# Attention-value matmuls issued between the two score matmuls of each exponential tile

## The reference, cut to what matters

```python
x = x + L0(x)        # a linear layer chosen by item
x = x + L1(x)        # a Laplacian in both directions and a reaction term
# L2, per item and head: 256 queries from the side input, 256 keys from x and one own key
score   = concat([q @ k_prev.T * SCALE (masked), (q * k_self).sum(-1) * SCALE])
weights = softmax(score)
attn    = weights[..., :-1] @ v_prev + weights[..., -1:] * v_self
x = x + attn @ Wo + bo
x = x + L3(x)        # three networks relu(x @ wi) @ wo, mixed by a softmax gate
```

## Time and profile before

| what | us |
|---|---|
| median of 3 runs | 1064.06 |
| lowest and highest run | 1061.18, 1064.1 |
| the profiled execution, its own time | 1063.02 |
| its span, first to last instruction | 1061.2 |

### The profile page before, as it was taken

One profiled execution on the slowest core, in us unless ns is written; L12 is line 12 of the kernel. 1 busy time (PEld: TensorE's weight loads), 2 busy tenths in 40 slices (PEclk: granted clock), 3 DMA queues, 4 the chain that ended last, 5 costly groups with the idle time before them and its releaser, 6 DMA issues.

```text
span 1061.2 us, 27596 instructions
## 1 busy us (share of the span) xinstructions
PE 990.0 (93%) x9488; PEld 931.2 (88%) x9488; DVE 795.0 (75%) x1552; ACT 682.1 (64%) x1435; POOL 616.8 (58%) x548
## 2 busy tenths in 40 slices
PE   5669999999999999999999999999999999999896
PEld 5359999898999989899998989999898999989896
DVE  6576787778878777887877788787778878778633
ACT  5564866667586666748666674866667486666641
POOL 5683747476474747647464664747566474755440
PEclk8669999999999999999999999999999999999988
DMA  6626142522514252251425225142522514251110
GB/s 161 166 83 109 51 70 76 94 80 60 109 50 67 76 96 80 60 109 50 66 77 96 80 59 107 53 64 77 98 80 59 109 51 62 78 98 52 42 50 11
DMA packets 91387, 82.68 MB, mean 78 GB/s; under 512 B 11972, under 2 KB 90852, under 8 KB 91364
## 3 DMA queue, kind: packets, MB, share of 16 engines
q1 hardware_dynamic: 91364, 82.38, 36.1%
HBM read 52.59 MB, written 4.20 MB: 54 GB/s over the span
## 4 chain that ended last, share of the span: by engine, by line
PE 65%; DVE 16%; issue 8%; ACT 7%; POOL 2%; DMA 1%; SPq 1%; DVEq 0%; ACTq 0%
PE hid L550 7%; PE hid L551 6%; PE hid L552 6%; PE out L550 6%; PE out L552 5%; PE out L551 5%; PE front L550 5%; PE front L552 4%; PE front L551 4%; PE front L652 4%; PE front L665 4%; DVE s_max L1034 3%; DVE hid_lo L1118 2%; DVE gate_terms L1133 2%; ACT prob L869 2%
## 5 line engine op out<-in xcount | busy, mean ns | idle before, releaser
L1269 POOL TENSOR_TENSOR prob_lo<-prob,prob_hi 128x512 f16<-128x512 f32 x144 | 175.1, 1216 | 102.9 <-ACT prob_hi L873 102.8
L550 PE MATMUL out<-hid_hi,exp_hi 128*128 128x256 f32 x768 | 228.5, 297 | 4.2 <-DVE hid_lo L1118 4.1
L550 PE MATMUL hid<-x_hi,exp_hi 128*128 128x256 f32 x768 | 230.3, 300 | 1.5 <-DVE x_lo L1114 1.5
L551 PE MATMUL hid<-x_lo,exp_hi 128*128 128x256 f32 x768 | 217.4, 283 | 0.0
L552 PE MATMUL hid<-x_hi,exp_lo 128*128 128x256 f32 x768 | 216.8, 282 | 0.0
L551 PE MATMUL out<-hid_lo,exp_hi 128*128 128x256 f32 x768 | 214.7, 280 | 0.0
L552 PE MATMUL out<-hid_hi,exp_lo 128*128 128x256 f32 x768 | 214.7, 280 | 0.0
L1212 POOL TENSOR_TENSOR exp_lo<-raw,exp_hi 128x512 fp32r<-128x512 f32 x128 | 169.1, 1336 | 70.6 <-ACT exp_hi L890 70.5
L1034 DVE TENSOR_REDUCE s_max<-front 128x2 f32<-128x512 f32 x256 | 167.9, 687 | 42.2 <-PE front L652 40.4
L869 ACT ACTIVATE prob<-front 128x512 f32<-128x512 f32 x256 | 154.2, 603 | 41.0 <-PE front L665 38.1
L1118 DVE SCALAR_TENSOR_TENSOR hid_lo<-hid,hid_hi 128x512 fp32r<-128x512 f32 x192 | 130.8, 681 | 62.8 <-ACT hid_hi L912 61.6
(11 more groups left out here) (166 smaller groups left out, 2266.5 us busy)
## 6 DMA issues: line engine op xcount, KB each, us to landing
raw<-in_wi SPq DMA_DIRECT2D x64, 256.0 KB, 3.8
raw<-in_wo SPq DMA_DIRECT2D x64, 256.0 KB, 2.8
q_rows<-w_raw SPq DMA_DIRECT2D x80, 128.0 KB, 4.0
k_rows<-x1T SPq DMA_DIRECT2D x48, 128.0 KB, 5.0
k_rows<-x_raw SPq DMA_DIRECT2D x48, 128.0 KB, 6.1
x_raw<-in_x SPq DMA_DIRECT2D x16, 256.0 KB, 2.9
w_raw<-in_w SPq DMA_DIRECT2D x16, 256.0 KB, 2.8
s_raw<-in_side SPq DMA_DIRECT2D x16, 256.0 KB, 3.7
```

What stands on the lines that cost most here:

```text
L550: nc.tensor.matmul(acc, w_hi, a_hi, start=first, stop=False)
L551: nc.tensor.matmul(acc, w_hi, a_lo, start=False, stop=False)
L1269: nc.gpsimd.tensor_tensor(prob_lo[:, h % NPROB, :], prob[:, h % NPROB, :], prob_hi[:, h % NPROB, :], ALU.subtract).then_inc(prob_split_poo ...
```

## The change

`attend` is called inside the loop over k, after the first of the two matmuls, and no longer after both. The increment that tells ACT that the head's scores are ready stays on the second matmul, which now comes after the eight matmuls of `attend` and after the waits at its head. The same instructions are issued, and the orders of ACT, DVE, POOL and SP are as before.

```diff
                     for k in range(C):
                         last = nc.tensor.matmul(psum[:, k * S:(k + 1) * S], k_rows[0:ROWS_EXP, h, k * P:(k + 1) * P],
                                                 q_rows[0:ROWS_EXP, h, :], start=True, stop=True)
+                        if k == 0 and h >= BEHIND:
+                            attend(i, h - BEHIND)
                 last.then_inc(filled[family(name)[0]], 1)
-                if name[0] == "E" and int(name[1:]) >= BEHIND:
-                    attend(i, int(name[1:]) - BEHIND)
```

## The result

The changed kernel takes **1084.66 us** (median of 4 runs, 1084.58 to 1084.71) against 1063.93 for the kernel before in the same comparison (1061.18 to 1064.10): ratio 1.0207, interval 1.0190 to 1.0223. It is 20.7 us slower. The profiled execution took 1084.64 us, its span is 1082.8.

What follows compares the result with a forecast made beforehand. It took a chain over ACT and DVE, alternating with TensorE, to bound the kernel. 1063.02 + 15 x 0.62 = 9.3, + 0.4 for turn 1, + 0 gave 1072.7, kept to 1073.0 us; range 1062 to 1078.0.

Steps and rivals of the forecast that it cites:

- What bounds the kernel: Whole turn: despite TensorE's 93% busy share, a chain over ACT and DVE ends later at three places where TensorE stops.
- TensorE sets the pace after all: Rival: `kp` need not wait, giving 1059.4 us, or 1052.2 if stops at `E11` and `P11` also move; chance 0.13.
- What TensorE saves: At nine E followed by a product, a wide matmul hides weight loading: 0.08 us each, 0.72 us a turn on TensorE.
- The sign I named: On TensorE, the step after `E4` and `E6` falls from 0.20 to 0.12 us if the prediction is right.
- What of it reaches the end: From the savings at `E4` and `E6`, 0 us a turn reaches the end, with bounds -0.16 to +0.13.
- reaches nobody: At most heads, scores 0.21 us later fall into an idle stretch of ACT and delay no one; `E11` is the exception.
- the term of `kp`: `kp` waits for the bank of `E11`: 0.62 us a turn over 15 turns, 9.3 us; bounds 0.52 to 0.8.
- What gets later, `kp`: `E11`'s scores reach ACT later, so `kp` starts at 504.63 instead of 504.01, 0.62 us a turn.
- The wait for `den`: Sign: TensorE's wait for DVE's `den`, at head 8 inside `E11`, stays and grows.
- Turn 1: At `E3`, ACT waits for head 0's value matmuls: 0.4 us once, between 0 and 0.6.
- It cancels: Rival: head 13's split on DVE shortens and savings at `E4` and `E6` pass, offsetting `kp`'s delay; 1062 to 1067, chance 0.09.
- a second chain opens: Rival: later scores also hold ACT at `E14` and `E15`, or `E7`, another 0.4 us a turn, 1079; chance 0.05.

Runs made afterwards that it cites:

- E4: Score step of head 4; the kernel before with `E4`, `E6` and `E12` alone changed: 1059.81 us against 1061.87, ratio 0.9976.
- E6: Score step of head 6; the kernel before with `E4`, `E6` and `E12` alone changed: 1059.81 us against 1061.87, ratio 0.9976.
- E12: Score step of head 12; the kernel before with `E4`, `E6` and `E12` alone changed: 1059.81 us against 1061.87, ratio 0.9976.
- E5: Score step of head 5; the kernel before with `E5` alone changed: 1077.18 us against 1061.87, ratio 1.0132.
- E11: Score step of head 11; the kernel before with `E11` alone changed: 1070.77 us against 1061.87, ratio 1.0074.
- E3: Score step of head 3; not run alone; whole change except at `E5` and `E11`: 1061.70 us against 1062.96, ratio 0.9988.
- the control: The kernel before with only `x_parts` moved ahead of `gate0` in DVE's order: 1062.14 us against 1063.32, ratio 0.9991.
- E14: Score step of head 14; not run alone; whole change except at `E5` and `E11`: 1061.70 us against 1062.96, ratio 0.9988.
- E15: Score step of head 15; not run alone; whole change except at `E5` and `E11`: 1061.70 us against 1062.96, ratio 0.9988.
- E7: Score step of head 7; not run alone; whole change except at `E5` and `E11`: 1061.70 us against 1062.96, ratio 0.9988.

## Why the prediction was right or wrong

**What bounds the kernel: right in the main.** TensorE is 91% busy, and taking 8.1 us off the busy time of its weight loads went along with 20.7 us more. The chain over ACT and DVE ends later at the stops, as the prediction read from the earlier trace rows. The rival *TensorE sets the pace after all* falls with that, at its full 10.8 us. In part it is borne out: with `E4`, `E6` and `E12` alone, where `kp` does not have to wait, it counted 1059.4, and 1059.81 came. Not borne out by its test is that DVE alone sets the piece from `kp` to `P11`: with `gate1` moved out of it, 0.08 a turn were gained, against a forecast of 0.5 to 1.0.

**What TensorE saves: right in size, with a badly chosen sign.** The sign I named, the step after `E4` and `E6` down from 0.20 to 0.12, did not come: after the change it reads 0.21 (500.59 to 500.80). But the last wide matmul now starts 0.23 ahead of that second product matmul, two steps of 0.11 and 0.12 with nothing between (timeline of PE: `E6`'s second matmul, then `H8`):

```profile
500.57 0.27 PE L665 MATMUL front<-q_rows,k_rows 100*128 100x256 bf16 x1
500.59 0.37 PE L550 MATMUL hid<-x_hi,exp_hi 128*128 128x256 f32 x1
500.80 0.28 PE L551 MATMUL hid<-x_lo,exp_hi 128*128 128x256 f32 x1
```

The product's first matmul is now recorded 0.02 behind the wide one, where a step between wide matmuls is 0.11 or more, so the step behind it does not show the saving. Over a longer stretch the saving is seen: from `E5`'s first matmul to the second of `H8` it took 1.06 us before (488.33 to 489.39), and takes 0.98 now (499.82 to 500.80), 0.08 less. And the run with `E4`, `E6` and `E12` alone shortens a turn by 0.23, 3 x 0.08.

**What of it reaches the end: this step failed.** It put the stretch of `E4` to `E6` at 0, with bounds of -0.16 and +0.13 a turn. It measured +0.90 in the whole change and +1.05 with `E5` alone. The prediction saw that DVE is nearly tied there and that `E5`'s scores come later by some 0.1 to 0.2 us; what it assumed is that such a delay can at most pass on whole. Just ahead of the two rows of DVE it looked at stood a small instruction with 0.18 us to spare against one on POOL, and `E5`'s delay of 0.15 to 0.21 cost 0.90 to 1.05 a turn. The sentence that at most heads the 0.21 "reaches nobody" fails with it: DVE waited for `E5`'s split already. The bound on DVE and POOL meeting differently was written into the term of `kp`, at 0.1 to 0.2, and not here. In sum this is 14 x 0.90 = 12.6 us, a little more than the 11.7 by which the forecast fell short (1084.7 less 1073.0). That the sign came out right is due to the term of `kp`, which holds by itself (`E11` alone), and not to luck.

**What gets later, `kp`: right.** Forecast 1.25 us from head 8 and 0.62 a turn, measured 1.24 and 0.61; the run with `E11` alone gives 8.9 us where the sum had 9.3. The new wait of TensorE stands 14 times, with 0.34 of recorded idle time where I had written about 0.5. The wait for `den` stayed and grew, 8.4 to 11.4.

**Turn 1: low.** 0.4 forecast. From `E3`'s start on TensorE to ACT's exponential it is 1.22 us before (48.94 to 50.16) and 1.94 after (49.54 to 51.48): 0.72 at the place named, against a bound of 0.6. That sum was done with durations of the full clock; here, in the windows from 40 to 60 us, the granted clock is 0.50 (1.2 GHz) before and after, with TensorE busy for 14.10 and 12.22 of the 20 us, and the eight value matmuls take 0.34 (50.71 to 51.05) instead of 0.21. The first 0.60 of the 1.7 by which head 8 is late is not the change's: in the control, with `E3` as it was, `E3` starts at 50.09, later still. Where the last 0.4 are from stays open.

**The other rivals.** *It cancels* did not come; *a second chain opens* is what happened, at 0.05 and 1079, but at the start of the turn through `E5`, and not at `E14`, `E15` or `E7`, where that rival put it.

## What to carry to other kernels

A matmul that signals another engine should not be put behind work that waits: move only those signals whose reader has slack, head by head, here three of thirteen. And in a tuned order, a delay of 0.2 us is not worth 0.2 us: before it is costed, list for each engine behind it the instructions that now start just ahead of a long one on the engine that shares its memory interface, and how much lead each has. A repair that pulls one stop forward wants the same list for the next stop.

## What was unexpected in the hardware

A small DVE instruction with two SBUF operands was held until the POOL instruction that had started just before it was done. The 128x8 `z_terms` took 0.17 us with a lead of 0.10 or 0.18 us over POOL's `s_lo` of 1.30 us, but 1.30 when it came 0.03 behind and 1.22 when it came 0.11 behind. POOL's `s_lo` took the same either way (1.29 and 1.30). A `TENSOR_SCALAR` that reads one large operand, 0.35 us alone, took 1.24 when it came 0.07 behind POOL's split of 1.17. The prediction knew such meetings only as the stretching of a long instruction; here the order of two starts, 0.1 us apart, decides over a whole microsecond. The description further up has it that engines wait for one another through semaphores only; this wait is one beside them. It ends with a POOL instruction that writes nothing that `z_terms` reads, and the profile counts it as busy time of DVE.
